# Attention scores in two row strips of the array, two groups of heads at a time

## The reference

```python
def attention(q, k, v):                       # q = layernorm(x), k = v = ctx
    Q, K, V = proj(q, Wq, bq), proj(k, Wk, bk), proj(v, Wv, bv)     # B, H=16, L=128, DH=8
    scores = einsum('bhid,bhjd->bhij', Q, K) / sqrt(DH)
    scores = scores + m[:, None, None] * softplus(1000 + |i - j|)   # one slope m for each head
    return einsum('bhij,bhjd->bhid', softmax(scores), V) @ Wo.T + bo
x = x + attention(layernorm(x), ctx, ctx)
x = x + experts(layernorm(x))    # top 2 of 16 experts of width 64, and a shared one of width 128
```

## Time and profile before

| | |
|---|---|
| median of 3 runs | 236.56 us (236.47 to 237.14) |
| profiled execution | 235.97 us, span of its instructions 234.2 us |
| TensorE busy | 213.8 us, 91% of the span |
| VectorE busy | 175.9 us, 75% |
| ScalarE busy | 118.3 us, 51% |
| GpSimd busy | 74.4 us, 32% |
| granted TensorE clock | 0.999 of full |

### The profile page before, as it was taken

One profiled execution on the slowest core, in us unless ns is written; L12 is line 12 of the kernel. 1 busy time (PEld: TensorE's weight loads), 2 busy tenths in 40 slices (PEclk: granted clock), 3 DMA queues, 4 the chain that ended last, 5 costly groups with the idle time before them and its releaser, 6 DMA issues.

```text
span 234.2 us, 6086 instructions
## 1 busy us (share of the span) xinstructions
PE 213.8 (91%) x1942; PEld 175.4 (75%) x1942; DVE 175.9 (75%) x612; ACT 118.3 (51%) x283; POOL 74.4 (32%) x178
## 2 busy tenths in 40 slices
PE   2969787979999999999999999999999899989995
PEld 2757455757788787977897878878897779768884
DVE  4599636995699678985899569957985788653891
ACT  8565656466426734475346443663367234763310
POOL 2500016010860159013921094107700580038000
PEclk9999999999999999999999999999999999999999
DMA  5553586223312470317032612325123600250000
GB/s 157 175 90 105 125 215 205 80 69 99 87 48 60 83 172 3 104 52 199 3 102 49 157 44 60 84 78 131 38 70 88 165 0 4 84 126 0 1 25 22
DMA packets 13079, 20.24 MB, mean 86 GB/s; under 512 B 2800, under 2 KB 9440, under 8 KB 12544
## 3 DMA queue, kind: packets, MB, share of 16 engines
q1 hardware_dynamic: 12080, 18.64, 31.2%
q10 hardware_dynamic: 976, 1.32, 1.8%
HBM read 16.03 MB, written 3.78 MB: 85 GB/s over the span
## 4 chain that ended last, share of the span: by engine, by line
issue 33%; PE 31%; DVE 17%; POOL 11%; ACT 3%; DMA 1%; DVEq 1%; ACTq 0%; POOLq 0%; SPq 0%
POOL hid L1314 6%; DVE nmax L971 6%; PE ps_up L511 5%; PE ps_pv L444 4%; PE ps_m L537 4%; PE ps_st L425 3%; PE ps_pv L451 3%; PE ps_up L516 2%; DVE tg L1075 2%; DVE stacks_sb L1202 1%; PE ps_up L308 1%; DMA ident<-in_c_ident 1%; DVE hid L1081 1%; PE ps_m L466 1%; POOL ve L1278 1%
## 5 line engine op out<-in xcount | busy, mean ns | idle before, releaser
L791 ACT ACTIVATE th<-ps_up 128x256 f32<-128x256 f32 x72 | 27.6, 383 | 35.5 <-PE ps_up L516 34.8
L735 ACT ACTIVATE probs<-ps_st 128x512 f32<-128x512 f32 x64 | 37.0, 595 | 16.3 <-PE ps_st L425 11.1
L537 PE MATMUL ps_m<-wd_sb,hid 128*128 128x128 f32 x288 | 44.8, 283 | 0.0
L971 DVE TENSOR_REDUCE nmax<-ps_s 128x4 f32<-128x512 f32 x64 | 41.9, 680 | 0.4 <-issue 0.4
L1075 DVE SCALAR_TENSOR_TENSOR tg<-th,ps_up 128x256 f32<-128x256 f32 x72 | 29.8, 414 | 13.5 <-ACT th L791 13.2
L1314 POOL TENSOR_TENSOR hid<-hid,crep 128x256 f32<-128x256 f32 x56 | 39.1, 732 | 0.2 <-issue 0.2
L537 PEld LDWEIGHTS ps_m<-wd_sb,hid 128*128 128x128 f32 x288 | 37.6, 191 | 1.0
L1081 DVE TENSOR_TENSOR hid<-tg,ps_up 128x256 f32<-128x256 f32 x72 | 29.7, 413 | 1.0
L511 PE MATMUL ps_up<-x_hi,wg_hi 128*128 128x256 f32 x72 | 26.6, 369 | 0.4 <-ACT x_hi L772 0.2
L1278 POOL TENSOR_TENSOR ve<-mv,eps_sb 128x1 f32<-128x1 f32 x16 | 3.0, 191 | 69.5 <-DVE mv L1022 69.5
L425 PE MATMUL ps_st<-stacks_sb 98*128 98x128 f16 x256 | 24.8, 220 | 0.2
(11 more groups left out here) (147 smaller groups left out, 434.2 us busy)
## 6 DMA issues: line engine op xcount, KB each, us to landing
crep<-cw_dram SPq DMA_DIRECT2D x28, 256.0 KB, 4.6
stacks_sb<-qk_dram SPq DMA_DIRECT2D x32, 128.0 KB, 3.4
qk_dram<-qk_parts SPq DMA_DIRECT2D x16, 128.0 KB, 1.8
out_y<-x_all SPq DMA_DIRECT2D x8, 128.0 KB, 4.6
wg_sb<-in_wgT ACTq DMA_DIRECT2D x1, 576.0 KB, 3.5
wu_sb<-in_wuT ACTq DMA_DIRECT2D x1, 576.0 KB, 3.3
wd_sb<-in_wd SPq DMA_DIRECT2D x1, 576.0 KB, 4.1
x_all<-in_x SPq DMA_DIRECT2D x2, 256.0 KB, 4.2
```

The lines of the kernel that those rows point to most:

```text
L537: last = mm(ps_dn[:, b * P:(b + 1) * P], hid[:, buf, c, b * P:(b + 1) * P], wd_sb[:, c, :], start=(c == 0 and b == 0), stop=(c == SHARED), ...
L735: fn(probs[:, b, g * HG * P:(g + 1) * HG * P], scores_bank(a, g)[:], ACT.Exp).then_inc(exp_sb, 1)
L791: fn(th[:, c % 2, :], ps_up[c % 2][:, 0, :], ACT.Tanh, scale=0.5).then_inc(tanh_sb, 1)
L971: v.tensor_reduce(nmax[:, b, HG * g:HG * g + HG], ps_s[g % 2][:].rearrange("p (h j) -> p h j", h=HG), AX_X, ALU.max, negate=True).then_inc ...
```

## The change

- The stack of a group is laid in two strips: heads 0 to 7 in partitions 0 to 33, heads 8 to 15 in 64 to 97, each with 32 rows of parts and 2 of the shift. The zero rows go, and with them the memsets that made them. A score product now takes 32 or 34 rows. The array is used in strips of 32 rows by `scores` and of 64 rows by `scores_T`.
- `scores` and `scores_T` make two groups at a time (`j` in place of `g`), one in each strip and bank, product by product in turn. They wait for all earlier maxima (or exponentials), so for both banks. Groups come in the order 0, 2, 1, 3.
- The bias of (0, 1) comes as a copy too, by VectorE: four of eight groups.
- The stack is loaded by 8 DMAs rather than 4, each half as large; the shift goes in two DMAs a row block rather than one. Before the keys' part SyncE also waits for `s_nm[0]`.
- The order is rewritten on TensorE, VectorE and ScalarE. Among others `qk_low(p, 1)` stands before `x2_low`, and `qk_low(p, 0)` right behind it; the wait on the values (`v_sb`) comes one group earlier.

```diff
                 for plane, row in ((2, 0), (3, 2 * DH)):
-                    src = bass.AP(qk_dram.tensor, (buf * 5 + plane) * (P * T), [[H * T, 2 * DH], [1, H * T]])
-                    sp.dma_start(stacks_sb[row:row + 2 * DH, buf, 1].rearrange("r h t -> r (h t)"), src).then_inc(s_stack, 16)
...
+                    for s in range(2):
+                        src = bass.AP(qk_dram.tensor, ((buf * 5 + plane) * P + s * HS) * T, [[H * T, 2 * DH], [1, HS * T]])
+                        at = STRIP * s + row
+                        sp.dma_start(stacks_sb[at:at + 2 * DH, buf, 1].rearrange("r h t -> r (h t)"), src).then_inc(s_stack, 16)
...
-            def scores(a, b, g, buf):
-                bank, n = ps_s[g % 2], 2 * NHG * a + NHG * b + g
-                if b == 0 and g == 0:
-                    pe.wait_ge(s_stack, 64 * a + 64)
+            def scores(a, b, j, buf):
+                n = 2 * NHG * a + NHG * b + 2 * j
+                if b == 0 and j == 0:
+                    pe.wait_ge(s_stack, 128 * a + 128)
+                    pe.wait_ge(v_sb, a + 1)
...
-                elif b == 0 and g == 1:
-                    pe.wait_ge(v_sb, a + 1)
                 else:
-                    pe.wait_ge(max_sb, n - 1)
-                if g == 0:
-                    mm(bank[:], dist16[:], slope_hi[:, 0:HG, :], start=True, stop=False, skip_group_check=True)
-                for h in range(HG * g, HG * g + HG):
-                    o = (h - HG * g) * P
-                    last = mm(bank[:, o:o + P], qs[buf][0:ZROWS, h, b * P:(b + 1) * P],
-                              ks[buf][0:ZROWS, h, b * P:(b + 1) * P],
-                              start=(g > 0), stop=True, skip_group_check=True)
-                last.then_inc(s_mm, 1)
+                    pe.wait_ge(max_sb, n)
+                if j == 0:
+                    mm(ps_s[0][:], dist16[:], slope_hi[:, 0:HG, :], start=True, stop=False, skip_group_check=True)
+                for k in range(HG):
+                    for s in range(2):
+                        row, h = STRIP * s, HG * j + k
+                        last = mm(ps_s[s][:, k * P:(k + 1) * P], qs[buf][row:row + SROWS, h, b * P:(b + 1) * P],
+                                  ks[buf][row:row + SROWS, h, b * P:(b + 1) * P], start=(j > 0 or s > 0), stop=True,
+                                  skip_group_check=True)
+                        if k == HG - 1:
+                            last.then_inc(s_mm, 1)
...
-            def scores_T(a, b, g, buf, f=None):
-                bank, n = scores_bank(a, g), 2 * NHG * a + NHG * b + g
-                seeded = not at_start(a) and (b, g) in ((0, 0), (1, 0), (1, 1))
+            def scores_T(a, b, j, buf, f=None):
+                n = 2 * NHG * a + NHG * b + 2 * j
+                seeded = not at_start(a) and True
                 if f is not None:
                     pe.wait_ge(lsh_sb, f + 1)
-                if at_start(a) and (b, g) == (0, 1):
+                if at_start(a) and b == 0 and j == 0:
                     pe.wait_ge(qklo_sb, 4)
-                if seeded and b == 0:
+                if seeded and b == 0 and j == 0:
                     pe.wait_ge(seed0_sb, a)
                 elif seeded:
-                    pe.wait_ge(seed1_sb, 2 * a + g - 1)
-                elif not (at_start(a) and b == 0 and g < 2):
-                    pe.wait_ge(exp_sb, n - 1)
-                if g == 0:
-                    pe.wait_ge(s_nm[b], 16 * a + 16)
+                    pe.wait_ge(seed1_sb, 3 * (a - 1) + 2 * b + j)
+                if not (at_start(a) and b == 0 and j == 0):
+                    pe.wait_ge(exp_sb, n)
+                if j == 0:
+                    pe.wait_ge(s_nm[b], 32 * a + 32)
...
-                first = False if seeded else bias(bank, g)[0]
-                for h in range(HG * g, HG * g + HG):
-                    o = (h - HG * g) * P
-                    last = mm(bank[:, o:o + P], ks[buf][:, h, b * P:(b + 1) * P], qs[buf][:, h, b * P:(b + 1) * P],
-                              start=first, stop=True, skip_group_check=True)
-                    first = False
-                last.then_inc(st_mm, 1)
...
+                first = [False if seeded else bias(scores_bank(a, 2 * j), ORDER[2 * j])[0],
+                         bias(scores_bank(a, 2 * j + 1), ORDER[2 * j + 1])[0]]
+                for k in range(HG):
+                    for s in range(2):
+                        row, h = STRIP * s, HG * j + k
+                        last = mm(scores_bank(a, 2 * j + s)[:, k * P:(k + 1) * P], ks[buf][row:row + AROWS, h, b * P:(b + 1) * P],
+                                  qs[buf][row:row + AROWS, h, b * P:(b + 1) * P], start=first[s], stop=True,
+                                  skip_group_check=True)
+                        first[s] = False
+                        if k == HG - 1:
+                            last.then_inc(st_mm, 1)
...
                 scores(a, 0, 0, abuf)
-                scores(a, 0, 1, abuf)
                 if p is not None:
                     project_q(p)
                     project_k(p)
                 late_down(0)
-                scores(a, 0, 2, abuf)
                 late_down(1)
                 expert_in_T(f)
-                scores(a, 0, 3, abuf)
+                scores(a, 0, 1, abuf)
                 late_down(2)
                 up(f, 0)
+                up(f, 1)
                 scores(a, 1, 0, abuf)
-                up(f, 1)
-                scores(a, 1, 1, abuf)
                 shift_T(a, 0)
                 router(f)
                 late_down(3)
-                scores(a, 1, 2, abuf)
                 up(f, 2)
+                scores(a, 1, 1, abuf)
                 late_down(4)
-                scores(a, 1, 3, abuf)
                 up(f, 3)
                 late_down(5)
-                scores_T(a, 0, 0, abuf)
+                scores_T(a, 0, 0, abuf, f=f)
                 late_down(6)
-                scores_T(a, 0, 1, abuf, f=f)
                 shift_T(a, 1)
                 late_down(7)
                 second_half(f, a, p, q, abuf)
             def second_half(f, a, p, q, abuf):
                 up(f, 4)
-                scores_T(a, 0, 2, abuf)
+                scores_T(a, 0, 1, abuf)
                 weights_T(f, a)
-                scores_T(a, 0, 3, abuf)
                 up(f, 5)
-                if not at_start(f): down(f - 1, (8,), abuf)
                 scores_T(a, 1, 0, abuf)
                 weigh_values(a, 0, f)
+                if not at_start(f): down(f - 1, (8,), abuf)
                 scores_T(a, 1, 1, abuf)
-                scores_T(a, 1, 2, abuf)
                 values_T(a, 0)
                 up(f, 6)
-                scores_T(a, 1, 3, abuf)
                 attention_T(a, 0, f)
...
             def shift_rows(a, b, buf):
                 act.wait_ge(nm_sb, 2 * a + b + 1)
-                act.dma_start(qs[buf][ZROWS:AROWS, :, b * P:(b + 1) * P], nmT[:, b, :]).then_inc(s_nm[b], 16)
+                for s in range(2):
+                    act.dma_start(qs[buf][STRIP * s + SROWS:STRIP * s + AROWS, :, b * P:(b + 1) * P],
+                                  nmT[H * s:H * (s + 1), b, :]).then_inc(s_nm[b], 16)
...
                 exponential(a, 0, 0)
                 shift_copy(a, 1)
                 shift_rows(a, 1, abuf)
+                exponential(a, 0, 1)
                 second_half(f, a, q)
             def second_half(f, a, q):
-                exponential(a, 0, 1)
                 tanh(f, 4)
                 exponential(a, 0, 2)
                 weights_copy(f)
...
-            def seed(a, g):
-                dve.wait_ge(exp_sb, 2 * NHG * a + NHG + g - 1)
-                v.tensor_copy(ps_st[(g + 1) % 2][:], bias_T[:, g, :]).then_inc(seed1_sb, 1)
+            def seed(a, g, b):
+                dve.wait_ge(exp_sb, 2 * NHG * a + (1 if b == 0 else NHG - 1 + 2 * g))
+                v.tensor_copy(ps_st[1][:], bias_T[:, g, :]).then_inc(seed1_sb, 1)
...
                     row_max(0, 0, g)
                 max_high(0, 0)
                 max_low(0, 0)
-                for g in range(NHG):
-                    row_max(0, 1, g)
+                row_max(0, 1, 0)
+                row_max(0, 1, 1)
+                qk_low(1, 1)
+                qk_low(1, 0)
+                row_max(0, 1, 2)
+                row_max(0, 1, 3)
                 max_high(0, 1)
                 max_low(0, 1)
-                qk_low(1, 1)
-                qk_low(1, 0)
...
                 if late:
                     gate(f - 1, 8)
                     hidden(f - 1, 8, abuf)
+                if p is not None: qk_low(p, 1)
                 x2_low(f)
+                if p is not None: qk_low(p, 0)
                 row_max(a, 0, 2)
                 row_max(a, 0, 3)
                 max_high(a, 0)
                 gate(f, 0)
                 max_low(a, 0)
                 hidden(f, 0, 1 - abuf)
-                if p is not None: qk_low(p, 1)
                 row_max(a, 1, 0)
-                if p is not None: qk_low(p, 0)
```

(9 more changed lines are left out.)

103 lines of the change are left out of this document (45 added, 58 removed).

## The result

| | before | changed kernel |
|---|---|---|
| median | 236.5 us | 262.0 us (260.4 to 263.3, 4 runs) |
| ratio | | 1.107, 95% interval 1.100 to 1.114 |
| profiled execution: span, granted clock | 234.2 us, 0.999 | 258.6 us, 0.954 |

A forecast was written before the change was run, and what follows sets the result against it. TensorE was taken to set the pace, VectorE close behind in a step's first half. Steps 10.1, first() 3.9, beginning 0.9 and end 0.5 summed to +15.4 us: 251.4 by the profiled execution, 252.0 beside the median; range 244 to 258.

The forecast's parts named there:

- rival 5: In the beginning, TensorE's clock falls to 1.2 GHz for two or three us, adding 1 to 2 us: 253.5; 3%.
- TensorE's work -0.73 us a step: Each step: 1.80 saved by overlapping strips and 0.38 by the bias copy, less 1.45 for layout changes and weight loads.
- rivals 2 and 3: Score products: strips don't overlap, +9 us, 260, 7%; or overlap in part, 0.29 us per eight, 255.6, 4%.
- `x_lo` +0.6: Each step: qk_low(p, 1), now ahead of x2_low on VectorE, delivers x_lo to TensorE later, +0.6 us.
- Both maxima +0.25: Each step: scores(a, 1, 0) waits for both maxima of the pair before, 0.55 us instead of 0.30.
- The pair (0, 1) behind two issues, +0.75: Each step: scores_T(a, 0, 1) waits for an exponential behind two DMA issues on ScalarE, taken at 0.47 each; +0.75 us.
- The seed of (1, 0) +0.5: Each step: scores_T(a, 1, 0) waits on TensorE for VectorE's bias copy seed(a, 0, 1), +0.5 us.
- `x2n` +0.25: Each step: TensorE reaches expert_in_T earlier with one product group less ahead, and waits 0.25 us more for x2n.
- The step +1.6: Each step: waits of +2.35 us and TensorE work of -0.73 make it 1.6 us longer.
- `first()` +3.9: In first(): waits for maxima, a second DMA issue, the second bank's bias and serial rounds add 3.9 us.
- The beginning +0.9: Before first(): eight stack loads replace four, the last issued 1.25 us later, so first scores start 0.9 us later.
- Rival 4: SyncE's eight stack loads delay expert weights, crep starts some 1.2 us later, 0.5 a step: 255.5; 13%.

The follow-up runs named there:

- e3_fill: The changed kernel with 24 + 8 + 10 + 6 more empty transposes in TensorE's queue of first(): 256.6 us.
- e2_exp_first: The changed kernel with, in first(), the first pair's exponentials ahead of the second shift's copy and issues, and exponential (0, 1, 1) ahead of the values' copy: 255.9 us.
- e14_fill_more: e3_fill with more empty transposes: 10 and 12 in the first step, 6 at the end of first(), 9 before the first step's expert_in_T: 255.0 us.
- e1_exp_step: The changed kernel with each step's exponential (a, 0, 1) ahead of the shift's copy and two DMA issues on ScalarE: 260.5 us.
- e5_qk_low: The changed kernel with the two qk_low back at their earlier places on VectorE, behind hidden(f, 0) and the first maxima of row block 1: 257.1 us.
- e6: The kernel before, with ScalarE issuing the shift rows of a row block as two DMAs instead of one: 241.9 us.
- e8_all: The changed kernel with exponentials ahead of issues and values' copy, empty transposes in first(), qk_low moved back, and the bias waiting only for its own bank's maxima: 246.7 us.
- e16_three_seeds: The changed kernel without its fourth bias copy: TensorE multiplies the bias of (0, 1) again, VectorE copies three a step: 262.6 us.
- e7_before_fourth_seed: The kernel before, with the bias of group 1 in row block 0 copied by VectorE instead of multiplied by TensorE: 245.3 us.
- e9_all_three_seeds: e8_all with the bias of (0, 1) multiplied by TensorE again, so three bias copies a step: 245.6 us.
- e13_best: e9_all_three_seeds with both shift issues of a step on SyncE's queue and 10 and 12 empty transposes in the first step: 246.5 us.

## Why the prediction was wrong in size

**What failed is rival 5, the clock.** I gave it 1 to 2 us and 3%, and nothing in the sum, with the reason "the stretch shown, and the whole page, stay at 1.00". That row tells only that a TensorE busy 98% of the time keeps its clock; it says nothing of a kernel that I myself had just given 3.9 us more in `first()`, mostly waits, and 2.35 us of waits in each step. What the runs show in its place, for the profiled execution: 3.7 us in `first()` (e3_fill), 1.5 in the fifth step (28.44 against 26.93 for the same step of e2_exp_first and e3_fill, which have no dip there), and 3.1 in the first step as the part of its +4.9 that the steps at full clock don't have. Of these 3.1, 1.6 to 1.75 are shown by runs with shorter dips in that step (27.19 in e2_exp_first, 27.04 in e14_fill_more); the other 1.3 or so are only argued (e1_exp_step had nearly as much low clock in its first step and was shorter). 8.3 us in all, where the whole excess over the forecast is 9.0 in this execution. The median of 262.0 is 1.5 above it, at lower clocks.

The other way round: the executions of e14_fill_more with one short dip (253.8 us), less the 1.5 to 2.2 that such a dip costs, leave an estimate of 251.6 to 252.3 for the changed kernel with an undisturbed clock. The forecast without the clock was 252.0. That it lies so near is in part luck: the beginning came 1.7 us earlier than forecast, and `first()` at full clock was 1.4 longer, the steps 0.1 to 0.3 each.

**Its other steps, by their own numbers.**
- TensorE's work -0.73 us a step: measured -0.71. Eight products in 0.225 us: L365 starts at 134.52 and the transpose behind it at 134.85; these 0.33, less the 0.09 of a layout change, are 0.24. The forecast held, rivals 2 and 3 did not. By the ratio that the Trainium skill gives in "TensorE: Matmul & The Clock Gate", Part 3, for four row strips it would have been 0.29 and 0.38; for two strips this trace doesn't show such a loss. The layout change into the strips: from the bias (134.20) it is 0.32 to the first product; a bias of 512 columns takes 0.22 by the columns of the earlier trace rows (896 in 0.38), which leaves 0.1, as forecast.
- `x_lo` +0.6: a wait of 0.44, and e5_qk_low gives back 0.4 to 0.8.
- Both maxima +0.25, from a wait of 0.30 to 0.55. The 0.30 of the earlier trace rows is the wait of the weight load, which comes with the matmul; the weight load at 134.20 has 0.58, so +0.28. (The matmul itself waits 0.38.)
- The pair (0, 1) behind two issues, +0.75: 1.11. The issue was mis-sized: 0.64 each, not 0.47. The single issue in the earlier trace rows has 0.62, and e6 shows too that half the data don't halve it (1.16 for two). I had 0.62 as the dear end.
- The seed of (1, 0) +0.5: 0.41. `x2n` +0.25: waits of 0.14 to 0.43 before L477 in the steps at full clock, where before had 0 to 0.18.
- Together +2.35 of waits: TensorE's idle time in a step rose by 2.16 (2.62 against 0.46). That the sum comes so near is because the pair (0, 1), 0.36 too low, made up for others that were too high. The step +1.6: 1.70 to 1.88.
- `first()` +3.9: 5.3 at full clock (24.64 against 19.39). Missed was ScalarE's order there: two exponentials behind two issues, and (0, 1, 1) behind the copy of the values. With both mended it is 23.8 with one short dip (e2_exp_first), so 22.2 to 22.3 without it by the 1.5 to 1.6 above, and 22.1 in e8_all, which also lets the bias go ahead of the second maxima. So the serial pairs cost some 2.8 and the order 2.5.
- The beginning +0.9: -0.8. The last of the eight was issued at 13.97, 1.4 later than the last before (I had 1.25), but its 64 KB landed 2.2 us after that, where the last 128 KB before took 4.4. The smaller loads more than made up for the later issue.
- Rival 4 did not happen: in the step from 127.49 the first DMA of `crep` is issued 19.6 us into the step, before 18.8 in the same one, but the step is 1.7 longer, and GpSimd starts its work right behind the normalisation, as in the earlier trace rows.
- The fourth bias copy "hidden in the second half, where VectorE has idle time" was right in its cost by e16_three_seeds, but not for that reason: VectorE stands still for 0.33 us only after the copy (at 143.15), and TensorE waits at that place for ScalarE. In the kernel before, where TensorE asks for that bank earlier and does not wait for ScalarE, such a copy costs 1.1 us a step and more (e7_before_fourth_seed).

Left open: why the clock falls in one step and not in its neighbours with the same waits, or in one run and not in another at the same place; why a dip costs more at one place than at another; and what the rest of +0.8 to +0.9 a step in e9_all_three_seeds is made of (its TensorE still waits for the shift's input, 0.2 to 0.6, and for the seed, 0.6 to 0.9; neither was taken away alone).

## What to carry to other kernels

When the trace of before shows one engine at 98%, ask also what one DMA issue or one copy more would do on the other queues: here 0.5 us more on ScalarE came through whole in each step, and a copy of 0.7 on VectorE cost 1.1 and more where TensorE had to wait for it. Handing over two buffers at once means that neither side can work on one while the other side has the other: it pays only if both have something else to do meanwhile. And idle time that a change gives to TensorE can have a second price in its clock, which a page at 1.00 doesn't show: add up the new idle time of a stretch before calling the clock safe. In a start-up without other work, empty matmuls can fill it, but only as many as there is idle time: where the wait is gone they are work like any other (the first step of e13_best).

## What the hardware showed unexpectedly

- Two row strips overlap (eight products in 0.24 us instead of 0.45) and don't need alternating instructions: with four products of one strip queued ahead of four of the other, the eight and the change behind them took 0.34 us, against 0.33 in turn.
- A DMA issue on ScalarE costs by the piece: 0.62 us for the rows of one shift, 1.16 to 1.28 for the same rows in two.
- Around an idle time of 2.8 us the clock went to half, and stayed there for 6.9 us of the 8 from 28 on, in which TensorE was busy for 5.2; a dip of about 3.4 us costs this kernel 1.5 to 2.2 us. In the change the fifth step has a dip (171 to 175) behind a single idle time of 1.11, which the steps beside it have too, without a dip.
- With the idle place before one dip filled, another can appear: with `first()` filled (e3_fill) the clock fell near 48 us, behind idle times of 0.7 and 1.05, where the change itself, with the same two idle times there, kept its clock until 59. Each of these is one profiled execution.
